# Cross-attention stream on one Trainium2 core: where a pair's first output matmuls stand on TensorE

## The reference

```python
def _L0_xattn_ref(query, key, value, cached_key, cached_value, in_proj_weight, in_proj_bias, ...):
    ...
    q = (jnp.einsum('bqe,fe->bqf', query, wq) + bq).reshape(B, Lq, H, D)
    k = (jnp.einsum('bke,fe->bkf', k_full, wk) + bk).reshape(B, Lkv, H, D)
    v = (jnp.einsum('bke,fe->bkf', v_full, wv) + bv).reshape(B, Lkv, H, D)
    scores = jnp.einsum('bqhd,bkhd->bhqk', q, k) * scale
    attn = jax.nn.softmax(scores, axis=-1)
    ctx = jnp.einsum('bhqk,bkhd->bqhd', attn, v).reshape(B, Lq, E)
    ...
x = x + _L0_xattn_ref(_layernorm(x, axis=-1), ctx_1024, ctx_1024, ctx_1024, ctx_1024, ...)
```

## Time and profile before

| what | value |
|---|---|
| runs | 1315.26, 1313.79, 1315.26 us; median 1315.26 |
| profiled execution | 1308.91 us, span of the trace 1307.2 us |
| TensorE (PE) busy | 1238.4 us, 95% of the span |
| VectorE (DVE) busy | 971.2 us, 74% |
| ScalarE (ACT) busy | 825.1 us, 63% |
| mean granted TensorE clock | 0.971 |

### The profile page before, as it was taken

How to read it: one execution, slowest core, us unless ns; L and a number is a source line. 1 busy time by engine, 2 the same in 40 slices (tenths; PEclk the granted TensorE clock), 3 DMA queues, 4 the chain that set the end, 5 groups by cost and what they waited for, 6 DMA issues and landing times. The chain is left out here.

```text
span 1307.2 us, 22711 instructions
## 1 busy us (share of the span) xinstructions
PE 1238.4 (95%) x9306; PEld 727.0 (56%) x9306; DVE 971.2 (74%) x852; ACT 825.1 (63%) x1085; POOL 147.1 (11%) x118
## 2 busy tenths in 40 slices
PE   5799999999999999999999999997768999999997
PEld 4555555555555555555555555552557666666664
DVE  6277777777777777777777777787745788787885
ACT  4476767777677777676776767665212665666663
POOL 0110101001011010110100101000002022221212
PEclk9899999999999999999999999999875999999999
DMA  4611011010010110101101000012602777877761
GB/s 166 189 34 33 2 33 33 1 33 8 27 33 2 33 33 1 33 1 33 33 1 33 5 30 1 1 29 85 243 18 85 267 254 250 246 246 244 242 202 57
DMA packets 56380, 107.91 MB, mean 83 GB/s; under 512 B 5875, under 2 KB 6003, under 8 KB 56273
## 3 DMA queue, kind: packets, MB, share of 16 engines
q1 hardware_dynamic: 53568, 101.55, 23.7%
q0 software_dynamic: 2720, 5.09, 1.7%
HBM read 95.57 MB, written 12.14 MB: 82 GB/s over the span
## 5 line engine op out<-in xcount | busy, mean ns | idle before, releaser
L498 DVE TENSOR_TENSOR p_sum<-p_sum,as_p 128x2048 f32<-128x2048 f32 x252 | 577.2, 2291 | 190.3 <-ACT as_p L465 189.5
L465 ACT ACTIVATE as_p<-as_s 128x1024 f32<-128x1024 f32 x512 | 496.1, 1022 | 122.9 <-PE as_s L394 122.8
L409 PE MATMUL as_o<-as_p,as_v 128*32 128x512 f32 x2048 | 247.1, 599 | 1.6 <-DVE o_acc L506 1.4
L346 POOL TENSOR_TENSOR as_c_lo<-as_c,as_c_hi 128x512 fp32r<-128x512 f32 x60 | 78.6, 1311 | 693.1 <-ACT as_c_hi L457 693.1
L394 PEld LDWEIGHTS as_s<-as_q_hi,as_k_hi 32*128 32x128 f32 x1024 | 49.4, 182 | 164.6 <-issue 152.1
L394 PE MATMUL as_s<-as_q_hi,as_k_hi 32*128 32x512 f32 x1024 | 129.6, 495 | 9.6 <-ACT as_p L465 8.8
L409 PEld LDWEIGHTS as_o<-as_p,as_v 128*32 128x32 f32 x2048 | 53.0, 109 | 125.0 <-issue 121.0
L394 PE MATMUL as_s<-as_q_lo,as_k_hi 32*128 32x512 f32 x1024 | 104.2, 392 | 0.0
L394 PE MATMUL as_s<-as_q_hi,as_k_lo 32*128 32x512 f32 x1024 | 104.0, 391 | 0.0
L1165 ACT ACTIVATE se_h<-se_ht,se_b_cur 128x128 f32<-128x128 f32 x128 | 36.5, 369 | 99.1 <-PE se_ht L1068 99.1
L1181 DVE TENSOR_TENSOR se_wi_lo<-ei_wi,se_wi_hi 128x2048 fp32r<-128x2048 f32 x32 | 73.3, 2291 | 30.9 <-ACT se_wi_hi L1143 30.9
(11 more groups left out here) (250 smaller groups left out, 1609.9 us busy)
## 6 DMA issues: line engine op xcount, KB each, us to landing
ei_wi<-w_in SPq DMA_DIRECT2D x32, 1024.0 KB, 6.7
ei_wo<-w_out SPq DMA_DIRECT2D x32, 1024.0 KB, 5.5
as_c<-ctx_t SPq DMA_DIRECT2D x16, 1024.0 KB, 5.3
slots_scratch<-as_zeros SPq DMA_DIRECT2D x10, 256.0 KB, 3.9
acc_scratch<-as_zeros SPq DMA_DIRECT2D x10, 256.0 KB, 3.9
pq_w<-xw_in SPq DMA_DIRECT2D x1, 2048.0 KB, 12.1
se_tokens<-slots_scratch SPq DMA_DIRECT2D x7, 256.0 KB, 5.4
x_sb<-x SPq DMA_DIRECT2D x4, 256.0 KB, 3.5
```

Of the source, the lines that this page charges most:

```text
L346: nc.gpsimd.tensor_tensor(c_lo[b][:, d, :], c[:, d, :], c_hi[b][:, d, :].bitcast(F32), ALU.subtract).then_inc(c_lo_ready, 1)
L409: last = nc.tensor.matmul(o[j * D:(j + 1) * D, :], v[b][:, t, feats], p[step % PR][:, j * NQ:(j + 1) * NQ], start=(t == 0), stop=(t == KT ...
L465: nc.scalar.activation(p[step % PR][:, pair * 2 * NQ:(pair + 1) * 2 * NQ], s[r][:, :], ACT.Exp, scale=SCALE).then_inc(p_ready[step % PR], 1)
L498: nc.vector.tensor_tensor(sums, sums, p[step % PR][:, :], ALU.add).then_inc(p_summed[step % PR], 1)
```

## The change

In a pair with a projection, O(2j-2) moves from behind S(2j+1) to in front of it, straight behind the projection. O(2j-1) stays where it was. Pairs without a projection keep their order. The programs of the other engines are the same.

```diff
                     if output_of(n, j):
                         bank_kept(n, j)
                         project(*output_of(n, j), proj[:, :])
-                    else:
-                        outputs_behind(n, 2 * j - 2)
+                    outputs_behind(n, 2 * j - 2)
                     scores(n, 2 * j + 1)
-                    if output_of(n, j):
-                        outputs_behind(n, 2 * j - 2)
                     outputs_behind(n, 2 * j - 1)
```

## The result

The changed kernel took 1371.36 us (median of four runs, 1368.75 to 1374.92) against 1314.53 us for the kernel before (1310.84 to 1315.26). The ratio is 1.0446, 95% interval 1.042 to 1.0472: slower. Between the medians that is 56.8 us more; by the ratio it is 58.6. The profiled execution took 1374.92 us, its span 1373.2.

What follows compares the result with a forecast made beforehand. TensorE was taken to bound the stage. A pair's 4.88 + 2.25 = 7.13 us against 6.64 gives 0.49 more, times 123 pairs 60 us, on a 1315.3 us median: 1375 us, range 1358 to 1390.

Steps and rivals of the forecast that it cites:

- The way from S(2j) to S(2j+1): TensorE, first to second scores of a pair: longer by one output's 1.00 us, 4.88 us against 3.88.
- The way to the next scores: TensorE, second scores to the next pair's: loses one output but waits for the exponential, 2.25 us, not 1.91.
- The parts of the sum: Each changed pair: 7.13 us against 6.64, 0.49 more, of which 0.15 extra seam and 0.34 wait; 60 us over 123 pairs.
- VectorE's move: Odd pairs: VectorE empties the output tile at 3.72 us, the moved output arrives at 3.88; 0.16 us left, no cost.
- Beside the stage: Outside the changed pairs: context loads get more time, pairs without projection and later stages stay, clock should stay at 1.00.
- rival of the seam alone: Changed pairs: only the extra change of tile shape costs, no wait; 18 us in all, 1333 us; chance 8%.

Runs made afterwards that it cites:

- the two runs with a long wait: On the changed kernel: VectorE's move out of the output tile one instruction later, 1537.42 us; the first outputs in front of the projection, 1604.95 us.

## Why the prediction was right

The forecast was 1375 us, and 1371.4 was measured; the growth was put at 60 us, and 56.8 was measured, between medians of runs that spread by 4 to 6 us; the way through the stage grew by 60.6 in the traces. Step by step:

1. *The way from S(2j) to S(2j+1)* was put at 4.88 and is 4.86 to 4.91. No row had shown outputs straight behind a projection; the trace after shows that this seam is like the others (2.98 from P to O, weights standing still for 0.36).
2. *The way to the next scores* was put at 2.25 and is 2.25 to 2.27. The pairs without a projection had shown it before the change was run. That it is the exponential and the ring is shown by four runs: half the exponential takes the wait away, the same cut does nothing in the old order, a ring of two brings a wait into the old order, and scores straight behind scores keep the same distance.
3. *The parts of the sum*, 0.15 for the seam and 0.34 for the wait, are 6.79 - 6.64 = 0.15 with the wait cut out, and 7.14 - 6.79 = 0.35.
4. *VectorE's move* was given 0.16 us of room; it has 0.13 (606.28 + 0.05 to 606.46). The even pairs alone cost half, so it costs nothing, as forecast. The later move shows that the room is all there is.
5. *Beside the stage*: the clock stayed at 1.00 in the stretch, as said. That held for waits of 0.3 us; it does not for 2.2. The step said nothing of the clock behind the stage, which differs from one execution to the next.

The rival of the seam alone had the seam's price right, 0.15 us of the 0.49, and nothing for the wait; with most of the waits cut out, the kernel took 18.3 us more than before. The count of seams is no measure of an order by itself: both outputs behind the projection have one change of shape fewer than the old order and cost 166.5 us. The Trainium skill, "TensorEngine Tiling (Array Packing)", Key Properties, says that changing the tiling mode drains TensorE; the weight loads' standstill of 0.36 us at each such change agrees with it.

What was off: the expectations for the two runs with a long wait, by 48 and 65 us. Most of each gap is the clock, which the sum of the waits did not hold.

None of the runs points to an order that beats the kernel before. In the old order the waits are covered and each step has one filler between its scores; scores without a filler would save a seam, but stand 2.27 us apart.

## What to carry to other kernels

Before work is moved out of a gap, ask what the gap covered: here the outputs behind the second scores filled the time that a three-deep PSUM ring needs (scores, exponential, signal: 2.26 us), and half of them were not enough. A stretch of the same kernel that already has the new order, the last chunk here, prices it better than any reasoning. A wait's own length is the lower bound of its price: look at the granted clock of the work behind it, which fell here after waits of 2.2 us in a third of the cases, and after waits of 1.29 us nowhere between 130 and 860 us.

## What the runs showed of the hardware that was not expected

TensorE's clock fell on waits of 2.2 us that came in every second pair, some 16 us apart: in 19 of 56 pairs, nearly always every third, the work behind the wait ran at 0.50 to 0.58 of full clock at first, and in the rest at 1.00, with the same idle time ahead of it (2.18 and 2.19 us in the two pairs shown). With waits of 2.78 us the clock fell in 37 of 55, in 18 of them only some way into the work. In the waits of some 0.3 us of the changed kernel, and of 1.29 us in every pair of the run with scores behind scores, the granted clock was 1.00 over the whole stretch from 130 to 860 us. What decides between the two kinds at the same wait was not tried.
